# Attention weights made from a second score product instead of by transposing: a fused attention and quantised-linear kernel

## What is computed

```
q = layernorm(x) @ w_q.T + b_q;  k, v = ctx @ w_k.T + b_k, ctx @ w_v.T + b_v
p = softmax(causal(q @ k.T / sqrt(32)))          per head, 256 x 256
x = x + tanh(g_xattn) * ((p @ v) @ w_o.T + b_o)
y = layernorm(x);  each 32 wide block of y and w_f is rounded to an fp6 grid times its scale
x = x + tanh(g_ffn) * (y_q @ w_fq.T + b_f)
```

## Time and profile before

| | |
|---|---|
| three runs | 1435.2 us median, 1435.06 to 1436.8 |
| the profiled execution | 1436.06 us |
| its span, first to last instruction | 1433.9 us |
| mean granted TensorE clock | 0.986 |
| busy: PE, DVE, ACT, POOL | 97%, 76%, 63%, 60% |

### The profile page before, as it was taken

One profiled execution on the slowest core, in us unless ns is written; L12 is line 12 of the kernel. 1 busy time (PEld: TensorE's weight loads), 2 busy tenths in 40 slices (PEclk: granted clock), 3 DMA queues, 4 the chain that ended last, 5 costly groups with the idle time before them and its releaser, 6 DMA issues.

```text
span 1433.9 us, 35255 instructions
## 1 busy us (share of the span) xinstructions
PE 1389.3 (97%) x10844; PEld 1225.0 (85%) x10844; DVE 1096.4 (76%) x4219; ACT 904.5 (63%) x2969; POOL 856.2 (60%) x1387
## 2 busy tenths in 40 slices
PE   6889999999999999999999999999999999999976
PEld 6778888888888888888888888888888888888855
DVE  6768787878778877778777778787777887777763
ACT  4666666666666666666666666666666666666651
POOL 2446665566665666665656666556666556666563
PEclk9999999999999999999999999999999999999997
DMA  8343344444434444433444443444343444443310
GB/s 255 106 117 99 101 107 118 115 128 106 118 91 115 118 125 117 108 97 108 120 118 123 108 113 93 119 115 127 102 124 87 115 118 126 115 113 85 88 54 30
DMA packets 156104, 159.12 MB, mean 111 GB/s; under 512 B 28176, under 2 KB 130576, under 8 KB 155920
## 3 DMA queue, kind: packets, MB, share of 16 engines
q1 hardware_dynamic: 155920, 156.87, 41.4%
HBM read 39.33 MB, written 16.78 MB: 39 GB/s over the span
## 4 chain that ended last, share of the span: by engine, by line
PE 93%; DVE 2%; issue 1%; SPq 1%; POOL 1%; DMA 1%; ACT 0%; DVEq 0%; ACTq 0%; POOLq 0%
PE proj L482 20%; PE proj L484 20%; PE proj L483 20%; PE pT_ps L532 13%; PE oT_ps L548 7%; PE proj L575 6%; PE s_ps L521 4%; PE s_ps L522 2%; SPq L341 1%; DMA all_probs<-in_L_xattn_w_v 1%; POOL x L443 0%; POOL x L447 0%; DVE all_probs L805 0%; SPq L321 0%; SPq L319 0%
## 5 line engine op out<-in xcount | busy, mean ns | idle before, releaser
L409 POOL TENSOR_TENSOR all_probs<-all_probs,rden 128x128 f32<-128x128 f32 (+1 forms) x1024 | 505.5, 515 | 483.2 <-DVE rden L865 481.2
L658 ACT ACTIVATE all_probs<-all_probs,neg_max 128x128 f32<-128x128 f32 (+1 forms) x1024 | 458.6, 450 | 410.2 <-DVE neg_max L805 410.0
L805 DVE CUSTOM_DVE_ANT_0 all_probs<-s_ps,causal 128x128 f32<-128x128 f32 (+1 forms) x1024 | 323.6, 353 | 213.4 <-PE s_ps L522 212.1
L532 PE MATMUL pT_ps<-ident,all_probs 128*128 128x128 f32 x1536 | 267.3, 284 | 3.1 <-ACT all_probs L736 1.9
L658 ACT ACTIVATION_READ_ACCUMULATOR all_probs<-all_probs,neg_max 128x1 f32 x1024 | 194.2, 190 | 0.0
L532 PEld LDWEIGHTS pT_ps<-ident,all_probs 128*128 128x128 f32 x1536 | 160.8, 142 | 30.2 <-issue 26.4
L917 DVE COPY all_probs<-pT_ps 128x384 f32<-128x384 f32 x256 | 140.3, 548 | 49.2 <-PE pT_ps L532 47.1
L521 PE MATMUL s_ps<-k_stack,q_stack 96*128 96x256 f32 x512 | 154.6, 302 | 0.8 <-DVE neg_max L805 0.8
L482 PE MATMUL proj<-cT_hi,wk_hi 128*128 128x256 f32 x512 | 154.2, 301 | 1.1 <-DVE cT_lo L859 1.1
L482 PE MATMUL proj<-aT_hi,wq_hi 128*128 128x256 f32 x512 | 147.4, 288 | 0.0
L483 PE MATMUL proj<-cT_lo,wk_hi 128*128 128x256 f32 x512 | 143.4, 280 | 0.0
(11 more groups left out here) (125 smaller groups left out, 3469.2 us busy)
## 6 DMA issues: line engine op xcount, KB each, us to landing
k_stack<-k_hi SPq DMA_DIRECT2D x512, 64.0 KB, 2.0
q_stack<-q_hi SPq DMA_DIRECT2D x512, 64.0 KB, 2.1
xs<-in_x SPq DMA_DIRECT2D x32, 512.0 KB, 4.4
cs<-in_ctx SPq DMA_DIRECT2D x32, 512.0 KB, 6.3
k_stack<-k_lo SPq DMA_DIRECT2D x256, 64.0 KB, 2.0
q_stack<-q_lo SPq DMA_DIRECT2D x256, 64.0 KB, 2.1
out<-x SPq DMA_DIRECT2D x32, 512.0 KB, 3.0
vs<-in_L_xattn_w_k SPq DMA_DIRECT2D x2, 512.0 KB, 6.4
```

What stands on the lines that cost most here:

```text
L409: last = nc.gpsimd.tensor_tensor(p, p, rden[:, sd, t, h:h + 1].to_broadcast([P, (1 + t) * P]), ALU.mult)
L532: last = nc.tensor.transpose(pT_ps[h % 2][:, m * P:(m + 1) * P], probs[:, h % P_RING, m * P:(m + 1) * P], ident[:, :])
L658: last = nc.scalar.activation(probs[:, h % P_RING, cols], probs[:, h % P_RING, cols], ACT.Exp, scale=-1.0, bias=neg_max[:, sd, t, h:h + 1] ...
L805: last = nc.vector.tensor_tensor_reduce(probs[:, h % P_RING, cols], s_ps[h % 2][:, cols], causal[:, (1 - t) * P:], 1.0, MASKED, ALU.add, A ...
```

## The change

The probabilities are no longer transposed, nor divided. The first scores serve for the maxima and the denominators alone: DVE's `maxima` and ACT's exponential with its sum stay (`denominators`), three places deep. For each group of four heads ACT then takes the logarithm of the denominators and an exponential of its negative (`logarithms`), and DVE makes the shift of each query, log of the denominator less `neg_max` with a correction, in high and low part, transposes this 32x32 block by block (`shift_rows`) and writes it as eight further rows, 96 to 103, beside q in the stack, by four copies (`shifts`). In k's stack these eight rows hold 0 and 1 (`choices`, once, at the start), choosing the head. Six slots after its first scores, PE makes a head's scores again with keys as rows and queries as columns, over 104 rows (`shifted_scores`), and ACT's exponential of them, 128x384 out of PSUM, is `probsT` (`weights_of_values`). POOL sets what is above the diagonal to zero (`triangles`, two blocks of 128x128 in one instruction). The values are weighed for eight heads at once, 32 matmuls, 15 slots after the first of the eight heads' scores, in slots 5 and 13.

q and k parts lie in one tile `qk`, both stacks in one tile `stack` with three places for eight heads, and one DMA fills both stacks' rows: 24 DMAs a batch, of twice the size. cT, k's first half and xT have lag 0, f has lag 3. x is normalised in its place and loaded a second time for the residual. The order of the units and of the slots of nearly all stages is new; which unit has its parts in which slot follows from `UNITS` and `SLOT_PARTS`:

Biases come as rows and are transposed on PE, the set-up of the weights stands in steps 0 and 1. The core of the diff:

```diff
-UNITS = [("cT", 0, 1), ("cT", 1, 1), ("q", 1, 2), ("dT", 0, 4), ("k", 0, 1), ("dT", 1, 4), ("f", 0, 4), ("xT", 0, 1),
-         ("f", 1, 4), ("xT", 1, 1), ("o", 0, 3), ("o", 1, 3), ("q", 0, 1), ("v", 0, 1), ("k", 1, 1), ("v", 1, 1)]
-BANKS = (0, 1, 2, 0, 1, 2, 0, 1, 2, 0, 1, 2, 0, 1, 0, 2)
+PAIR = 2 * GROUP
+S_SLOT = SLOTS + 6
+T_LAG = 6
+AV_LAG = 15
...
+UNITS = [("o", 0, 3), ("q", 0, 1), ("o", 1, 3), ("k", 1, 1), ("v", 0, 1), ("cT", 0, 0), ("v", 1, 1), ("cT", 1, 0),
+         ("q", 1, 1), ("dT", 0, 3), ("k", 0, 0), ("dT", 1, 3), ("f", 0, 3), ("xT", 0, 0), ("f", 1, 3), ("xT", 1, 0)]
 PARTS = {"cT": 1, "xT": 1, "dT": 1, "q": 4, "k": 4, "v": 4, "o": 4, "f": 4}
-SLOT_PARTS = (2, 4, 4, 1, 1, 5, 4, 2, 3, 4, 4, 1, 3, 3, 3, 2)
...
+SLOT_PARTS = (3, 3, 3, 3, 3, 1, 3, 3, 3, 4, 3, 3, 3, 1, 4, 3)
+BANKS = 3
+STAGES = 4
...
+P_RING = 3
+PT_RING = 10
+R_RING = 2
...
+        def again_head(g):
+            n = g - S_SLOT - T_LAG
+            return n if 0 <= n < N_HEADS else None
+        def shift_group(g):
+            m, rest = divmod(g - S_SLOT - GROUP, GROUP)
+            return m if rest == 0 and 0 <= m < N_HEADS // GROUP else None
+        def value_block(g):
+            a, rest = divmod(g - S_SLOT - AV_LAG, PAIR)
+            return a if rest == 0 and 0 <= a < N_BLOCKS else None
...
+                    its = slice(j * DK, (j + 1) * DK)
+                    at = n % 3 * PAIR + 2 * j
+                    for r, (q_at, k_at) in enumerate(((0, 0), (1, 0), (0, 1))):
+                        k_at += 2 + 2 * half
+                        src = qk[its, q_at:k_at + 1:k_at - q_at]
+                        sp.dma_start(stack[r * DK:(r + 1) * DK, :, at:at + 2, :].bitcast(F32),
+                                     src.bitcast(F32)).then_inc(stacked[n % 3][j], 16)
...
-            def divide(b, h, sd):
-                pool.wait_ge(rden_ok, HEADS * b + h + 1)
-                for t, cols in enumerate((slice(0, P), slice(P, 3 * P))):
-                    p = probs[:, h % P_RING, cols]
-                    last = nc.gpsimd.tensor_tensor(p, p, rden[:, sd, t, h:h + 1].to_broadcast([P, (1 + t) * P]),
-                                                   ALU.mult)
-                last.then_inc(div_ok, 1)
...
+            def triangles(n):
+                pool.wait_ge(pT_ok, n + 1)
+                p = probsT[:, n % PT_RING, :].rearrange("p (a q) -> p a q", a=3)[:, 0:3:2, :]
+                nc.gpsimd.affine_select(out=p, in_=p, compare_op=ALU.is_ge, fill=no, base=0,
+                                        pattern=[[0, 2], [1, P]], channel_multiplier=-1).then_inc(tri_ok, 1)
...
-            def transpose_probs(b, h):
-                pe.wait_ge(div_ok, HEADS * b + h + 1)
-                if some(n := 8 * b + h // 2):
-                    pe.wait_ge(pT_odd if h % 2 else pT_even, n)
-                for m in range(3):
-                    last = nc.tensor.transpose(pT_ps[h % 2][:, m * P:(m + 1) * P],
-                                               probs[:, h % P_RING, m * P:(m + 1) * P], ident[:, :])
-                last.then_inc(pT_done, 1)
...
+            def shifted_scores(n):
+                bank = sT_ps[n % 2]
+                if n == 0:
+                    pe.wait_ge(choice_ok, 1)
+                if n % GROUP == 0:
+                    pe.wait_ge(shift_ok, n // GROUP + 1)
+                if n >= 2:
+                    pe.wait_ge(pT_ok, n - 1)
+                h = place(n)
+                nc.tensor.matmul(bank[:, 0:S], stack[:, 1, h, 0:P], stack[:, 0, h, :], start=True, stop=True)
+                nc.tensor.matmul(bank[:, S:S + P], stack[:, 1, h, P:S], stack[:, 0, h, P:S], start=True,
+                                 stop=True).then_inc(sT_done, 1)
...
+            def weigh_values(a):
...
+                if a:
+                    pe.wait_ge(olo_ok, a)
+                else:
+                    pe.wait_ge(wlo_ok, KC * len(WEIGHTS))
+                for m in range(2):
+                    for kt in range(T):
+                        for j in range(GROUP):
+                            d = (PAIR * r + GROUP * m + j) * DK
+                            last = nc.tensor.matmul(
+                                oT_ps[j * DK:(j + 1) * DK, m * S + kt * P:(m + 1) * S], vs[:, b % 2, kt, d:d + DK],
+                                probsT[:, (PAIR * a + 2 * j + m) % PT_RING, 2 * P * kt:2 * P + P * kt], start=kt == 0,
+                                stop=kt == T - 1, tile_position=(0, j * DK))
                 last.then_inc(av_done, 1)
...
+            def denominators(n):
+                G, h = divmod(n, GROUP)
                 act.wait_ge(max_ok, n + 1)
                 for t, cols in enumerate((slice(0, P), slice(P, 3 * P))):
-                    last = nc.scalar.activation(probs[:, h % P_RING, cols], probs[:, h % P_RING, cols], ACT.Exp,
-                                                scale=-1.0, bias=neg_max[:, sd, t, h:h + 1],
-                                                accum_out=den[:, sd, t, h:h + 1])
-                last.then_inc(p_ok, 1)
-            def unit(u, kind, half, b, sd):
-                bank = proj[BANKS[u]]
+                    last = nc.scalar.activation(probs[:, n % P_RING, cols], probs[:, n % P_RING, cols], ACT.Exp,
+                                                scale=-1.0, bias=neg_max[:, G % R_RING, t, h:h + 1],
+                                                accum_out=den[:, G % R_RING, t, h:h + 1])
+                last.then_inc(den_ok, 1)
+            def logarithms(G):
+                act.wait_ge(den_ok, GROUP * (G + 1))
+                nc.scalar.activation(ln_den[:, G % R_RING, :, :], den[:, G % R_RING, :, :], ACT.Ln).then_inc(ln_ok, 1)
+                act.wait_ge(ln_ok, G + 1)
+                if G:
+                    act.wait_ge(r_ok, 2 * G)
+                nc.scalar.activation(near_one[:, :, :], ln_den[:, G % R_RING, :, :], ACT.Exp,
+                                     scale=-1.0).then_inc(exp_ok, 1)
+            def weights_of_values(n):
+                act.wait_ge(sT_done, n + 1)
+                if n >= PT_RING:
+                    act.wait_ge(av_done, (n - PT_RING) // PAIR + 1)
+                nc.scalar.activation(probsT[:, n % PT_RING, :], sT_ps[n % 2][:, 0:3 * P], ACT.Exp,
+                                     scale=-1.0).then_inc(pT_ok, 1)
...
+            def shifts(G):
+                its = G % R_RING
+                dve.wait_ge(max_ok, GROUP * (G + 1))
+                dve.wait_ge(ln_ok, G + 1)
+                nc.vector.tensor_tensor(bare, ln_den[:, its], neg_max[:, its], ALU.subtract).then_inc(bare_ok, 1)
+                dve.wait_ge(exp_ok, G + 1)
+                nc.vector.tensor_tensor(near_one[:, :, :], near_one[:, :, :], den[:, its], ALU.mult).then_inc(bare_ok, 1)
+                dve.wait_ge(bare_ok, 2 * G + 2)
+                if G:
+                    dve.wait_ge(rows_ok, G)
+                nc.vector.scalar_tensor_tensor(shift, near_one[:, :, :], -1.0, bare, ALU.add,
+                                               ALU.add).then_inc(r_ok, 1)
+                nc.vector.scalar_tensor_tensor(shift_cols[:, :, 0:GROUP].bitcast(F32R), near_one[:, :, :], -1.0,
+                                               bare, ALU.add, ALU.add).then_inc(r_ok, 1)
+                dve.wait_ge(r_ok, 2 * G + 2)
+                nc.vector.tensor_tensor(shift_cols[:, :, GROUP:SHIFT].bitcast(F32R), shift,
+                                        shift_cols[:, :, 0:GROUP], ALU.subtract).then_inc(cols_ok, 1)
+                dve.wait_ge(cols_ok, G + 1)
+                if G:
+                    dve.wait_ge(shift_ok, G)
+                nc.vector.transpose(shift_rows[:, :, :].rearrange("p t c -> p (t c)"),
+                                    shift_cols[:, :, :].rearrange("p t c -> p (t c)")).then_inc(rows_ok, 1)
+                dve.wait_ge(rows_ok, G + 1)
+                if G >= 6:
+                    dve.wait_ge(sT_done, GROUP * (G - 5))
+                at = place(GROUP * G)
+                for e in range(GROUP):
+                    to = stack[ROWS:, 0, at:at + GROUP, :].rearrange("c h (t e l) -> c h t e l", t=T, e=GROUP)[:, :, :, e]
+                    rows = shift_rows[e * DK:e * DK + SHIFT, :, :].unsqueeze(1).to_broadcast([SHIFT, GROUP, T, DK])
+                    last = nc.vector.tensor_copy(to, rows)
+                last.then_inc(shift_ok, 1)
...
-            def reciprocals(b, h, sd):
-                dve.wait_ge(p_ok, HEADS * b + h + 1)
-                nc.vector.reciprocal(rden[:, sd, :, h], den[:, sd, :, h]).then_inc(rden_ok, 1)
```

More of the change, by code:

```diff
@@ L95, in live @@
     def live(b):
-        return not isinstance(b, int) or 0 <= b < B
-    def at(i, n):
-        return isinstance(i, int) and i == n
-    def some(n):
-        return not isinstance(n, int) or n > 0
+        return 0 <= b < B
     with ExitStack() as es:
@@ L253, in blocks, with finished @@
             return a.rearrange("p (n w) -> p n w", w=FP6_BLOCK)
-        def column(b):
-            return b.rearrange("(c p) -> p c", p=P)
```

(50 more changed lines are left out.)

682 lines of the change are left out of this document (337 added, 345 removed).

## The result

The changed kernel takes 1624.2 us (median of 4 runs, 1616.7 to 1625.1) against 1435.7 in the runs of the kernel before beside it: a ratio of 1.130, 95% interval 1.127 to 1.133. The forecast was 1414 with a range of 1362 to 1472. The profiled execution is 1625.1, its span 1623.0.

A forecast was written before the change was run, and what follows sets the result against it. PE bounded the kernel at 42.59 us a step; afterwards a loop through PE and DVE would. 29 steps of 42.3, 130 of other work, 55 idle and 2.2 outside the span gave 1414 us, range 1362 to 1472.

The forecast's parts named there:

- The loop: PE waits for DVE's dT0 low part, DVE for PE's scores of slot 2: 42.3 us a step with hand-overs.
- rival 2: Slower through the shift block on DVE, once a block passes 2.0 us: 1448, or 1492 at its dearest; chance 0.38.
- A block is 1.8: One shift block on DVE: small instructions 0.9 us plus four copies 0.9; bounds 1.4 to 2.5.
- Four copies ... half of that is 0.22: 0.9: The shift block's copies of 256 elements on DVE, priced at half of a 128x512 instruction's 0.45 us.
- its normalising twice 0.45: DVE's normalising of x between slots 2 and 11: two instructions of 0.45 us each.
- the lock: Port pair shared by DVE and POOL: it could hold up nearly all the shift block's instructions; the sum included no such wait.
- Stalls cost PE its clock ... Folded into the range: Rival on PE's clock: five or six stalls a step, each under 1.2 us; no chance of its own.
- PE's term, 39.75: PE's own work a step after the change, without waits: 39.75 us, down from 42.6.
- 0.09 more: Extra us of the first matmul behind a head's transposes on PE, counted in the 0.35 a head removed.
- rival 1: PE stays the bound, with steps of 39.75 to 41.4 us: 1340 to 1388 in total; chance 0.17.
- I take 55 of idle: Idle time at the kernel's start and end after the change: 55 us, 45 to 70, with a shorter tail.
- a block counts about four times: A shift block enters a step's loop three times directly and once more by the maxima behind it.

The follow-up runs named there:

- pool_away: The changed kernel with POOL's four adds of 128x512 a step moved three and two slots later: 1633.5 us, ratio 1.138.
- rows_on_pool: The changed kernel with the shift block's four copies made by POOL instead of DVE, x's instructions left in place: 1655.8 us, ratio 1.153.

## Why the prediction was wrong, point by point

- **The loop was the right mechanism.** PE's waits are at the places it named: the shift rows, cT's low part, dT. Taking DVE's work out of slots 2 to 11 brings the step back (47.7 to 42.2). Measured in one step, DVE's leg from the maxima of slot 2 (806.89) to the end of dT0's low part (837.31) is 30.4 us, where the terms give 25.1 + 1.8 + 0.3 = 27.2; PE's leg, 837.46 to 854.03, is 16.6 and not 14.2. What failed is the size of terms, and so even rival 2 at its dearest, 1492, was 132 too low.
- **The failed step, first term: "A block is 1.8".** It is 2.44 in the step shown, 2.4 on average. The small ones were right (1.03 for 0.9). "Four copies ... half of that is 0.22: 0.9" was wrong: 0.30 each when alone, and one in every second block held by POOL to about 0.5, so 1.2 to 1.4. The 128x512 row that I halved is no copy but the normalising (L881), and times do not halve with the elements: in the earlier trace rows a TENSOR_SCALAR of 128x512 takes 0.53 and one of 128x16 still 0.15. The copy also repeats its source for each head and writes another type; what each of these costs no run shows. My upper bound of 2.5 had it, with "0.4", and the chance of 0.38 on rival 2. Three blocks: 1.9 of the 5.4 us that a step is over.
- **Second term: "its normalising twice 0.45".** 1.9 instead of 0.9. I weighed the lock for the block alone, where it did little (L795 0.19 on average for 0.15 alone, a copy 0.31 for 0.29), and not for the instruction that stands beside POOL's adds in the new order: 1.0.
- **Third: "Stalls cost PE its clock ... Folded into the range".** It was about 1.5 us a step, some 40 in all by the 24 stretches, two of them double. The argument was that each stall would be under 1.2 us; the one at dT became 1.9 on average, as the first two terms fell into it. These three are 4.4 of the 5.4; most of the other 1.0 is PE's leg beyond the clock's part, 16.6 - 14.2 - 1.5 = 0.9, where the next point falls in.
- **PE's term, 39.75, was too low by 1.8, hidden by the loop.** "0.09 more" for the first matmul behind the transposes was booked as removed, and the second pair as 0.18. The 0.05 behind a short matmul stays, and there is another behind each new one: 0.10 x 16 = 1.6 by the rows; the run without second scores saw 0.3 to 0.7 of it, as their part. So rival 1's 1340 was never to be had, and without any block the change is still 0.7% slower.
- **"I take 55 of idle".** The edges hold 1623.0 - 29 x 47.7 = 240, where before had 199 and the forecast 185. Of the 41 over before, 15 are three steps' worth at the dearer rate; the tail is 8.6 longer (51.8 for 43.2), the first scores are 5.8 later, and the other 12 lie in the slower filling of the pipeline, which the kernel without the block shows too (17.6 over the first 42 heads). I had expected the tail shorter, since f comes earlier; the shift's way made it longer.
- **Right:** rows cost nothing; no reloading of function tables; ACT and POOL not bounds (33.2 and 17.9 for a forecast of 32 and 19); DMA issues hidden but for 0.4 a step of PE's waits. In rival 2's rule, "a block counts about four times", 0.64 gives 2.6, three quarters of which the block itself explains.

## What to carry to other kernels

When a change moves work from an engine that is full to one that is 80% busy, write out the loop through both and price each new instruction by a row of its own form, or take the upper bound: here every 0.1 us taken out of a block gave some 0.5 a step, as one late link brought a longer stall, a collision with POOL's adds and a stretch at half clock. Before giving a removed instruction the wait seen behind it, ask whether the instruction that now comes last there brings the same one. And run the change with its cost left out: 1446 against 1435 says that mending the shift block alone can't make this order pay.

## What was not expected of the hardware

- A score matmul over 96 or 104 rows costs PE about 0.11 us, whether 128 or 256 columns stream (step 41.99 against 42.38 with twice 16 of them doubled); of a short one 0.05 stands in the next instruction's row.
- With waits of PE of 1.6 to 2.9 us comes a stretch of 3.4 us at half clock, a loss of about 1.5, but not always: with 20 of 21 in the changed kernel, 8 of 21 in pool_away, 10 of 21 in rows_on_pool. With each wait of 6.0 us came one of 6.8, a loss of 2.0. In the kernel with x later, where PE's longest wait is 1.7 and those at xT at most 1.3, there is none in a middle step.
- DVE's normalising of 128x512 takes 0.55 us alone and 1.5 beside a 128x512 add of POOL, and moving the adds moves the loss to a 128x8 instruction (0.19 to 0.44 on average) and to the copies (0.31 to 0.38). Instructions of DVE that read PSUM, and a TENSOR_REDUCE within SBUF (0.68), keep their time beside POOL's instructions of that size.
- A copy of only 8 partitions by 256 elements takes DVE 0.285 at best and POOL 0.40.
